# Third convolution of a four-layer network kernel: offset taps on VectorE, key taps on GpSimd, normalising and copying on ScalarE

## The reference, cut to what matters

```python
value = dwconv(x, w_v, b_v, 1)            # depthwise 3x3, padding 1
query = dwconv(x, w_q, b_q, 1)
key   = dwconv(x, w_k, b_k, 2)            # stride 2: 8 x 8 pixels
off   = dwconv(x, w_off1, b_off1, 2)
o = gelu(layernorm_over_channels(off) * ln_g + ln_b)
pos = tanh(einsum('bhwc,pc->bhwp', o, w_off2) + ref)
v_sampled = grid_sample_bilinear(value, pos[..., ::-1])
attn = einsum('bcm,bcn->bmn', query, key) * SCALE      # 12 heads of 32 rows
out  = einsum('bmn,bcn->bcm', attn, v_sampled)
y    = einsum('bchw,oc->bohw', out, w_out)
```

## Time and profile before

| | us |
|---|---|
| median of 3 runs | 1338.05 (1337.55 to 1339.08) |
| the profiled execution's own time | 1337.37 |
| its span, first to last instruction | 1335.4 |
| granted TensorE clock, mean | 0.93 of full speed |
| PE busy / DVE busy / ACT busy / POOL busy | 1174.9 / 821.3 / 475.6 / 244.2 |

### The profile page before, as it was taken

One profiled execution on the slowest core, in us unless ns is written; L12 is line 12 of the kernel. 1 busy time (PEld: TensorE's weight loads), 2 busy tenths in 40 slices (PEclk: granted clock), 3 DMA queues, 4 the chain that ended last, 5 costly groups with the idle time before them and its releaser, 6 DMA issues. The chain is left out here.

```text
span 1335.4 us, 23843 instructions
## 1 busy us (share of the span) xinstructions
PE 1174.9 (88%) x8364; PEld 1018.0 (76%) x8364; DVE 821.3 (62%) x2962; ACT 475.6 (36%) x922; POOL 244.2 (18%) x227
## 2 busy tenths in 40 slices
PE   2979999948999997999996999997999968997675
PEld 2978888937999996888894767676888967886454
DVE  6137676556666653767655666545767667777775
ACT  3523333314455543334331222224433312331322
POOL 3002212122010101121214243222121212111000
PEclk9989999967999997999996999997999978999777
DMA  3201010010000000000000000000000000000000
GB/s 136 75 24 49 13 47 0 0 48 1 1 2 1 2 1 1 1 1 0 0 1 0 1 1 1 1 1 1 1 0 0 0 1 1 1 1 0 0 19 30
DMA packets 11561, 15.67 MB, mean 12 GB/s; under 512 B 7385, under 2 KB 9007, under 8 KB 11346
## 3 DMA queue, kind: packets, MB, share of 16 engines
q1 hardware_dynamic: 10754, 12.86, 3.0%
q10 hardware_dynamic: 720, 1.66, 0.3%
HBM read 11.37 MB, written 3.15 MB: 11 GB/s over the span
## 5 line engine op out<-in xcount | busy, mean ns | idle before, releaser
L663 PEld LDWEIGHTS moe_dn<-all_w,moe_hid 128*128 128x128 f32 x2304 | 270.1, 192 | 5.9
L663 PE MATMUL moe_dn<-all_w,moe_hid 128*128 128x96 f32 x2304 | 271.5, 275 | 0.0
L600 ACT ACTIVATE moe_hid<-moe_up 128x512 f32<-128x512 f32 x288 | 169.7, 598 | 233.9 <-PE moe_up L655 221.8
L653 PE MATMUL moe_up<-moe_xh,moe_w1h 97*128 97x512 f32 x288 | 124.1, 431 | 0.0
L558 DVE SCALAR_TENSOR_TENSOR all_X<-moe_dn,moe_gate,all_X 128x96 f32 (+1 forms) x384 | 95.1, 310 | 33.4 <-PE moe_dn L663 29.1
L655 PE MATMUL moe_up<-moe_xl,moe_w1h 97*128 97x512 f32 x288 | 115.7, 402 | 0.0
L654 PE MATMUL moe_up<-moe_xh,moe_w1l 97*128 97x512 f32 x288 | 115.5, 401 | 0.0
L550 DVE SCALAR_TENSOR_TENSOR all_X<-all_b,moe_gate,all_X 128x96 f32 (+1 forms) x384 | 96.6, 314 | 10.8 <-DVE all_X L558 7.8
L481 POOL TENSOR_TENSOR moe_prob<-moe_euler,moe_logit 128x16 f32<-128x16 f32 x24 | 69.6, 2902 | 141.6 <-DVEq L517 141.6
L1060 PE MATMUL l1c_o<-l1c_vs,l1c_pt 128*128 128x64 f32 x768 | 94.4, 277 | 0.8 <-DVE l1c_ro L853 0.8
L1060 PEld LDWEIGHTS l1c_o<-l1c_vs,l1c_pt 128*128 128x128 f32 x768 | 91.8, 195 | 3.2 <-issue 1.4
(11 more groups left out here) (331 smaller groups left out, 2013.1 us busy)
## 6 DMA issues: line engine op xcount, KB each, us to landing
all_w<-w SPq DMA_DIRECT2D x3, 582.0 KB
all_w<-w SPq DMA_DIRECT2D x3, 576.0 KB
all_X<-x_rows SPq DMA_DIRECT2D x2, 768.0 KB, 6.8
conv_scratch<-all_X SPq DMA_DIRECT2D x2, 768.0 KB, 3.2
all_X<-conv_scratch SPq DMA_DIRECT2D x2, 768.0 KB, 4.8
out_tokens<-l3f_y SPq DMA_DIRECT2D x5, 288.0 KB, 2.1
l0c_band<-band ACTq DMA_DIRECT2D x1, 1248.0 KB, 9.3
all_b<-b SPq DMA_DIRECT2D x3, 192.0 KB
```

Of the source, the lines that this page charges most:

```text
L600: act.activation(hid[:, n, :], up[n % UPS][:, :], ACT.Gelu).then_inc(hid_done, 1)
L653: pe.matmul(bank, w1h[:, n, :], xh[:, p, :], start=True, stop=False)
L663: last = pe.matmul(dn[e % 2][:, j * C:(j + 1) * C], hid[:, n, j * P:(j + 1) * P], w2[:, n, :], start=(k == 0), stop=(k == KC - 1))
```

## The change

The offsets' nine taps go to VectorE (`offset_taps`), the keys' to GpSimd (`key_taps`: products of three taps a row into a buffer `kt`, summed afterwards). Both compute 17 rows of 8, two images one above the other with a row between them. Only the queries stay on TensorE. `normalise`, `offset_norm` and `values_out` move to ScalarE, as activations with a scale and a shift; GpSimd computes the shift (mean times reciprocal deviation, sign reversed) with one more small product. `turn_offsets` becomes two plain matmuls with the identity. The orders of the rounds change with it.

```diff
+            def window(p, t, stride):
+                rows = KROWS if stride == 2 else ROWS
+                dy, dx = t // KS, t % KS
+                return xp[:, p % 2, dy:dy + stride * (rows - 1) + 1:stride, dx:dx + SIDE:stride]
...
+            def key_taps(p):                                             # GpSimd
+                wait(pool, S["xp_done"], p + 1)
+                wait(pool, S["kb_done"], 2 * p)
+                for dy in range(KS):
+                    rows = xp[:, p % 2, dy:dy + 2 * KROWS - 1:2, :]
+                    wide = rows.rearrange("c y (x s) -> c s y x", s=2)
+                    pool.tensor_tensor(kt[:, dy, 0:2, :, :], wide[:, :, :, 0:KSIDE],
+                                       spread_tap(KS * dy, 2), ALU.mult)
+                    ins = pool.tensor_tensor(kt[:, dy, 2, :, :], wide[:, 0, :, 1:KSIDE + 1],
+                                             spread_tap(KS * dy + 2, 1).squeeze(1), ALU.mult)
+                chain.sync(ins)
+                chain.sync(pool.tensor_tensor(kt[:, 0, :, :, :], kt[:, 0, :, :, :], kt[:, 1, :, :, :], ALU.add))
+                chain.sync(pool.tensor_tensor(kt[:, 0, :, :, :], kt[:, 0, :, :, :], kt[:, 2, :, :, :], ALU.add))
+                pool.tensor_scalar(kt[:, 0, 2, :, :], kt[:, 0, 2, :, :], bias[:, 1:2], None, ALU.add)
+                chain.sync(pool.tensor_tensor(kt[:, 0, 0, :, :], kt[:, 0, 0, :, :], kt[:, 0, 1, :, :], ALU.add))
+                chain.sync(pool.tensor_tensor(key[:, :, :], kt[:, 0, 0, :, :], kt[:, 0, 2, :, :], ALU.add))
...
             rstd_of(0)
-            make_diag(pool, 1)
-            make_diag(pool, 0).then_inc(S["diag_kq"], 1)
             rstd_of(1)
             for p in range(NP):
+                key_taps(p)
+                keys(p, 0)
                 offsets_rstd(p)
                 if p in (0, 2):
                     rstd_of(2 + p // 2)
-                for i in range(2):
-                    keys(p, i)
+                keys(p, 1)
...
+            def offset_taps(p):                                          # VectorE
+                wait(dve, S["xp_done"], p + 1)
+                wait(dve, S["on_in"], p)
+                chain.sync(dve.tensor_scalar(off[:, :, :], window(p, 0, 2), taps[:, 2, 0:1], bias[:, 2:3],
+                                             ALU.mult, ALU.add))
+                for t in range(1, TAPS):
+                    ins = dve.scalar_tensor_tensor(out=off[:, :, :], in0=window(p, t, 2), scalar=taps[:, 2, t:t + 1],
+                                                   in1=off[:, :, :], op0=ALU.mult, op1=ALU.add)
...
             for p in range(NP + 2):
+                if live(p):
+                    offset_taps(p)
                 if live(p - 2):
                     add_output(p - 2, 0)
-                if live(p):
-                    value_taps(p, 1, 5)
-                if live(p - 2):
                     add_output(p - 2, 1)
                 if live(p):
+                    value_taps(p, 1, 3)
                     offset_moments(p)
-                    value_taps(p, 5, 6)
-                    offset_norm(p)
-                if live(p - 1):
-                    values_out(p - 1)
-                if live(p):
-                    value_taps(p, 6, TAPS)
+                    value_taps(p, 3, 5)
                 if live(p - 1):
                     sampled_out(p - 1, 0)
-                if live(p + 1):
-                    normalise(p + 1)
+                if live(p):
+                    value_taps(p, 5, 7)
                 if live(p - 1):
                     sampled_out(p - 1, 1)
+                if live(p):
+                    value_taps(p, 7, TAPS)
...
             for p in range(NP + 1):                                      # TensorE
-                if live(p):
-                    conv_offsets(p)
                 if live(p - 2):
                     project(p - 2, 1)
                 if live(p - 1):
                     scores(p - 1, 0)
                     scores(p - 1, 1)
-                if live(p):
-                    turn_offsets(p)
-                    if p == 0:
-                        pe.wait_ge(S["diag_kq"], 1)
-                    conv_keys(p)
                 if live(p - 1):
                     turn_values(p - 1)
                 if live(p):
+                    turn_offsets(p)
                     conv_queries(p, 0, 4)
```

More of the change, by code:

```diff
@@ L1279, in token_moments @@
                 moments(stats[:, part, :], diff[:, part], mean[:, part], var[:, part], 1e-6)
[L1280 to L1289 removed]
+                dve.tensor_scalar(shift[:, part], mean[:, part], -1.0, None, ALU.mult).then_inc(S["var_done"], 1)
             def offset_moments(p):
@@ L1371, in tokens_out @@
                 wait(act, S["val_done"], p - 1)
+                wait(act, S["kb_done"], 2 * (p - 2) + 1)
                 act.activation(images(p)[:, :, 1:SIDE + 1, 1:SIDE + 1],
@@ L1380, in first_tap, with normalise, offset_norm, values_out @@
                                ACT.Identity, scale=taps[:, 3, 0:1], bias=bias[:, 3:4]).then_inc(S["tap_done"], 1)
-            def offsets_out(p):
-                wait(act, S["off_in"], p + 1)
-                wait(act, S["on_in"], p)
-                act.activation(off[:, :], off_ps, ACT.Identity, bias=bias[:, 2:3]).then_inc(S["off_out"], 1)
-            def keys_out(p):
-                wait(act, S["k_in"], p + 1)
-                wait(act, S["kb_done"], 2 * p)
-                act.activation(key[:, :, :].rearrange("c i n -> c (i n)"), k_ps, ACT.Identity, bias=bias[:, 1:2]
-                               ).then_inc(S["k_out"], 1)
+            def normalise(p):
+                wait(act, S["rstd_done"], next(n for n, (lo, hi) in enumerate(BATCHES) if 4 * p < hi) + 1)
+                wait(act, S["turned"], p - 1)
+                for t in range(4):
+                    n = 4 * p + t
+                    ins = act.activation(xn[:, p % 2, t, :], X[:, n, :], ACT.Identity, scale=rstd[:, n:n + 1],
+                                         bias=shift[:, n:n + 1])
+                ins.then_inc(S["xn_done"], 1)
+            def offset_norm(p):
+                wait(act, S["orstd_done"], p + 1)
+                wait(act, S["og_in"], p)
+                act.activation(on[:, :], on_ps, ACT.Identity, scale=orstd[:, 0:1], bias=oshift[:, 0:1]
+                               ).then_inc(S["on_done"], 1)
+            def values_out(p):
+                wait(act, S["vt_in"], p + 1)
+                wait(act, S["vb_in"], 2 * p)
+                act.activation(vt[:, :, :, :].rearrange("p i t c -> p (i t c)"), vp[:, 0:4 * C], ACT.Copy
+                               ).then_inc(S["vt_out"], 1)
             def queries_out(p):
@@ L1431, in _ @@
             act.wait_ge(S["consts"], 2)
+            normalise(0)
             tokens_out(0)
@@ L1439, in _ @@
                     scores_out(p - 1, 1)
+                    values_out(p - 1)
                 if live(p):
-                    keys_out(p)
+                    offset_norm(p)
                     activated(p)
+                if live(p + 1):
+                    normalise(p + 1)
+                if live(p):
                     hats(p)
@@ L1489, in turn_offsets @@
             def turn_offsets(p):
-                wait(pe, S["off_out"], p + 1)
-                pe.transpose(on_ps, off[:, :], ident[0:C, 0:C]).then_inc(S["on_in"], 1)
+                wait(pe, S["off_done"], p + 1)
+                wait(pe, S["th_done"], p)
+                for i in range(2):
+                    o = off[:, PAD // 2 * i:PAD // 2 * i + KSIDE, :].rearrange("c y x -> c (y x)")
+                    ins = pe.matmul(fp[KPIX * i:KPIX * (i + 1), 2 * KP2:2 * KP2 + C], o, ident[0:C, 0:C],
+                                    start=True, stop=True)
+                ins.then_inc(S["on_in"], 1)
             def turn_back(p):
```

101 lines of the change are left out of this document (39 added, 62 removed).

## The result

The changed kernel takes 1377.28 us (median of 4 runs, 1370.99 to 1381.48), the kernel before 1337.82: the ratio is 1.0281 (95% interval 1.0261 to 1.0302). It is slower, as forecast. By the medians the difference is 39.5 us; the other 6 us lie in executions of which no trace was kept.

What follows compares the result with a forecast made beforehand. TensorE was taken to bound the kernel. From 1337.4 us: start -1.9, p = 1 -1.4, p = 2 to 7 +9.6, low clock +24.9, late moments +1, giving 1369.6, by the median 1370; range 1342 to 1386.

Steps and rivals of the forecast that it cites:

- 27 to 28 us: Sign expected in the new profile: length of the stage's rounds, with the low clock included.
- The wait for the add: TensorE's first projection waits for VectorE's add behind nine offset taps, a stop of 5.7 us, in p = 2 to 7.
- strict alternation: VectorE's offset taps and GpSimd's products take turns, one tap to one product; taps with the first and a signal 5.8 us.
- A round without the clock: A round of p = 2 to 7 takes 18.2 + 5.9 = 24.1 us, 1.6 more than before: +9.6 us.
- The clock: TensorE's granted clock falls to 0.50 after each stop, in seven rounds: +24.9 us (ends 15.4 and 33.6).
- I take 9: Length in us of the low-clock stretch after each TensorE restart, between 5.6 and 12.2.
- Nothing is lost there: At turn_back: offsets_rstd, though behind GpSimd's key taps, comes no later than its input, so TensorE does not wait.
- The smaller edits: Normalising and copies on ScalarE: -1.9 us at the start, hidden in later rounds; +1 for late moments at p = 2.
- (a): Rival: the clock holds through TensorE's stops; +7.3 us, 1345 us; chance 0.08.
- (b): Rival: taps slip through beside GpSimd in 3.3 us, TensorE restarts at xp_done + 3.75, clock holds; 1328 us; chance 0.10.
- (c): Rival: the taps slip through beside GpSimd, but the clock falls; +11 us, 1349 us; chance 0.07.
- (d): Rival: VectorE and GpSimd each wait for the other's whole instruction; taps take 8.3 us; 1385 us; chance 0.05.

Runs made afterwards that it cites:

- e1: The changed kernel with add_output(p-2, 0) put back ahead of offset_taps(p) in VectorE's order; 1362.32 us, ratio 1.0172.
- e3: The changed kernel with GpSimd's key_taps(p) also waiting until VectorE's nine offset taps are through; 1375.12 us, ratio 1.0278.
- e2: The changed kernel with ten extra matmuls of 256 columns, not used in the output, ahead of project(p-2, 1) in rounds 2 to 7; 1360.06 us, ratio 1.0157.
- e7: e1 with two query taps ahead of turn_offsets, offsets_rstd ahead of the keys products, later tokens' deviations behind the next round's keys; 1360.55 us, ratio 1.0161.
- e9: The kernel before with only normalise, offset_norm and values_out moved to ScalarE, with GpSimd's product for the shift; 1337.88 us, ratio 0.9996.
- e11: e5 with the later tokens' reciprocal deviation behind the bilinear products on GpSimd and values_out ahead of offset_norm on VectorE; 1319.4 us, ratio 0.9856.
- e12: The kernel before with only the offsets' taps moved to VectorE, behind add_output(p-2, 0); 1341.8 us, ratio 1.0008.
- e13: e7 with the first two query taps at the head of TensorE's round, ahead of project(p-2, 1); 1337.74 us, ratio 0.9990.
- e8: e5 with the later tokens' reciprocal deviations on GpSimd moved behind the keys of the round after; 1327.05 us, ratio 0.9911.
- e14: e13 with the later tokens' moments moved behind the moments of the offsets in VectorE's rounds of pairs 1 and 3; 1335.22 us, ratio 0.9974.
- e5: The kernel before with only the keys' taps moved to GpSimd, the offsets' convolution kept on TensorE; 1327.94 us, ratio 0.9919.
- e10: e7 with eight extra matmuls of 256 columns ahead of the scores in rounds 1 to 7, their result overwritten; 1359.57 us, ratio 1.0148.

## Why the prediction was right

Mechanism and sign are as forecast; that the size came out is in part luck. By rounds, the 33.6 us are: start -1.8; p = 0 -0.2; p = 1 +4.9; p = 2 to 6 +3.2, +5.4, +3.1, +7.2, +2.8; p = 7 and all behind it +8.9. The forecast had -1.9, 0, +2.1, five times 5.1 and 1 for the moments, and 5.1. So p = 2 to 7 cost some 3 us less than forecast, p = 1 2.7 more, and 2.0 lie behind the stage, where the forecast had nothing and where the code did not change. The forecast's 1370 is 7 us below the median. No round took the "27 to 28 us" that it named: they are of 25.3 to 25.7 or of 29.1 to 29.7, and p = 2 to 6 have a mean of 27.1. And one of its own signs of being wrong, TensorE waiting at turn_back, came in two rounds. In its steps:

- **The wait for the add** is as forecast in its place, its releaser and its six rounds; e1, which takes away only that, confirms it. Its size was 4.76, not 5.7 us. The first tap took 0.41 in place of 0.3, the eight others 4.41 in place of 5.5: 0.55 each. The price of a lone tap, 0.34, was right (354 ns at least, 362 the median in e3), and so was "strict alternation": the six products of the keys take 0.56 us each from the first start to the last end (814.54 to 817.90), and the six taps that start between them 0.55 each (814.77 to 818.05). What was too dear is the product. The shortest of its two forms take 635 and 411 ns:

```profile
L1243 POOL TENSOR_TENSOR l2c_kt<-l2c_xp,all_l_taps x24: 635/692/1151, 712.5 to 897.3; 96x272 f32<-96x272 f32 x24
...
L1245 POOL TENSOR_TENSOR l2c_kt<-l2c_xp,all_l_taps x24: 411/478/915, 713.1 to 898.0; 96x136 f32<-96x136 f32 x24
```

  That is 0.52 on average, where the estimate had 0.74 and 0.53; 0.36 + 0.52 - 0.31 = 0.57 is what is seen. And the first two of the eight, beside the last bilinear products, took 1.13 us (813.64 to 814.77) in place of 1.48.
- **A round without the clock** is 23.2 us (e2), where the forecast had 24.1: 0.9 too much in each of the steady rounds.
- **The clock** was the largest term, and the mechanism is shown by e2 (17 us back by nothing but keeping TensorE busy). The seven low stretches are 75.0 us, 10.7 each, but the forecast counted from the restart, and TensorE was busy in only 58.5 of them: 8.4 each, close to "I take 9". Only the one of p = 1 was like that, though: of the two of 17.1 us 13.9 and 13.5 are behind the restart, beyond the upper end of 12.2, and of the three of 6.8 us only 4.7 to 5.5, a little below the lower end of 5.6. Against the same rounds of e2, the low clock cost 2.1 to 2.5 us in p = 2, 4 and 6 and 6.4 and 6.2 in p = 5 and 7, 3.9 on average where the forecast had 3.6. So the stop, 0.9 too dear, and the low clock, 0.3 too cheap, cancel in part.
- **"Nothing is lost there"** at turn_back is wrong in two rounds: 2.73 us in p = 1 and 1.91 in p = 3. GpSimd's timeline of the latter:

```profile
785.23 2.27 POOL L1226 TENSOR_TENSOR l2c_rstd<-l2c_var,l2c_mhalf 128x12 f32<-128x12 f32 x1 [11.71 <-DVE l2c_shift L1309]
...
789.32 2.88 POOL L1263 TENSOR_TENSOR l2c_bil<-l2c_hat 128x256 f32<-128x256 f32 x4
792.15 0.64 POOL L1243 TENSOR_TENSOR l2c_kt<-l2c_xp,all_l_taps 96x272 f32<-96x272 f32 x1
...
802.36 0.56 POOL L1231 TENSOR_TENSOR l2c_orstd<-l2c_ovar,l2c_mhalf 128x1 f32<-128x1 f32 x1
803.00 1.14 POOL L1232 TENSOR_TENSOR l2c_oshift<-l2c_oshift,l2c_orstd 128x1 f32<-128x1 f32 x1
```

  GpSimd stands 11.7 us before a deviation whose moments come last in VectorE's round; the bilinear products and the key taps are queued behind it. The bilinear ones begin 5.3 us after xp_done (784.05), not 1.4 before it, and the key taps 8.1 us after it, not 1.4. The prediction counted GpSimd's round from a start that it has only in the other rounds. The order supports it: in e7, where the deviations stand further back, no wait of over 0.3 us is left at turn_back. In p = 1 the wait of 2.9 us that it put at the taps was 0.60 there and 1.56 for the keys' kb, and with the 2.73 at turn_back and a low stretch of 10.2 us this gives +4.9 instead of +2.1 (+9.4 in e1 and e2, see there).
- **The smaller edits**: -1.8 at the start, for -1.9; the move to ScalarE is free (e9), though its four tiles take 1.53 us in a round where the sum had 1.35.
- **The end**: p = 7 has a low stretch of 17.1 us and is 7.0 us longer, much as p = 5 is; the rounds that drain the pipeline take the same as before. The other 2.0 of the 8.9 us lie behind the stage. There the code is that of before, and its time is between 430.9 and 433.8 us in all the traces, the changed kernel's being 433.4 and before's 431.4; what decides this is open.

Of the rivals, (a) and (b) fall with the low clock in every round, and (b) and (c) with the taps, which took 4.9 us, not 3.3, so that TensorE went on at xp_done + 5.3, not 3.75. (d), each blocked for the whole of the other's instruction, falls too: it had 8.3 us for the taps, and a pair would cost 0.36 + 0.52 = 0.88 where it costs 0.57.

The Trainium skill's rule behind (d) (SBUF — State Buffer, "Who interferes with whom") is borne out in that the two engines take turns, and not in its measure: a pair needs some 0.31 us less than its two instructions alone in this trace, as in the earlier trace rows.

What lies behind the sign: the change is two that work against each other. The keys' half alone wins 1.4% once two orders are mended (e11). The offsets' half alone changes nothing (e12), and both halves together were nowhere faster than the keys alone, though their steady rounds at full clock are the shortest (19.67 in e7 and e13, against 20.15 in e11). The offsets are needed at the head of a chain that ends in the next `xp_done`, where the convolution takes 2.33 us and the nine taps 3.6 (e12), 3.9 (e3), 4.9 (the changed kernel) or 5.6 (e7). The two halves also went to different engines; no run tells what that alone makes.

Open: what decides how long the clock stays low, and whether it falls after a wait of under 2 us. The runs only order it: with the offsets' convolution at the head of a round, with two taps of the queries there, or with the keys' convolution behind the scores, it held in the steady rounds of the traces; with none of these (e1, e7) it fell in three of four.

## What to carry to other kernels

Before moving work off the engine that bounds, look for what stands behind the moved work in the new engine's order and is awaited by the old one: here a 0.34 us add behind nine taps. A stop of TensorE can cost its length and the low clock behind it, here 2.1 to 6.4 us for a stop of 4.8, so a move that shortens its work but opens one stop a round can lose; take first the part whose result is needed late (the keys), and put an instruction that waits for a late input where that input is ready, not in front of work that could already run (e11; in e8 and e14, moved elsewhere, it only shifted the wait).

## What the runs showed that was not expected

- The clock fell with waits of 1.90 us (e1), and in e7 in rounds whose waits at the head were 0.31 and 0.54 us; it held after one of 3.03 (e5) and one of 1.91 (e1, the round of 22.11). The length of the stop alone does not decide it.
- In the steady part of the stage low stretches lasted 3.4, 6.8, 10.2, 13.7, 17.1 or 24 us, the last with TensorE busy in all of it (e14); the longest that the forecast had was 12.2.
- A matmul of 256 columns in f32 costs 0.40 us at full clock (e10), three times what had been put down for it.
